# Graph network of four layers on one core: order of the closing units, the engine of the row checks, the place of four low halves, and the order of 16 bias matmuls

## The chip, the cores and the metric

One core of a Trainium2 chip. The metric is the device time of one execution in microseconds, the median of three runs. TensorE (PE) does the matmuls, VectorE (DVE) and ScalarE (ACT) empty PSUM and do the elementwise work, GpSimd (POOL) does elementwise work between SBUF tiles, and SyncE (SP) issues the DMAs.

## What is computed

`x` has 8 batches of 2048 nodes with 64 features. `adj` is a 2048 x 2048 matrix with the same value in all non-zero places of a row (each row is divided by its count). Each of four layers has the form `x = layernorm(x + f(x, adj))`:

```
# layer 0: weights and bias of each node from an embedding of 16 numbers
w = einsum('nd,dkio->nkio', embedding, weight);  b = einsum('nd,do->no', embedding, bias)
x_g = (x, A x, 2 A (A x) - x);                   out = einsum('bnki,nkio->bno', x_g, w) + b
# layer 1: attention over adj > 0.5; layer 2: (A + I)(x W' + b) / degree
# layer 3: three steps of v = relu([v, A v] W1' + b1) W2' + b2, then the last layernorm
```

## The kernel before

**Data.** `X` holds the nodes in 16 tiles of 128 rows, with four column chunks `c` of 128 (two batches each). A unit (c, j) is a chunk and four node tiles, 128 x 512 values. `Bm` holds the pattern of `adj` in fp8, in 2 x 16 tiles of 128 x 1024: the left columns first, then the right ones. Matmuls take each value as two f16 halves. The high half is written by ACT and the low half by DVE (helper `lo_half`, line 1190 in the profile) or POOL.

**Order.** The whole program is one list of steps, `HEAD + MIDDLE + TAIL`, written by hand. Each engine walks the same list and does its own part of each step, so within an engine the list sets the order, and between engines semaphores do. `last_order` builds the last part with `at(k, ...)`, work beside product k, and `on(h, ...)`, work ahead of half slot h. `between` puts work between the two quarters of a half slot.

**Head.** While `adj` arrives, `tensor_head` multiplies all 16 left tiles into eight PSUM banks (lines 795 to 802). Then step `("R", jt)` makes DVE turn right tile jt into the pattern (`edges`, line 1187). Step `("E1", n)` has ACT write the high half of left unit n (line 1009) and DVE the low half. Product `P1` (`quarter`, line 743) takes unit 8 and later: its quarter q waits for right tiles up to 4q + 3, and its first quarter also for the low half that frees its bank. `("nb",)` is 16 f32 matmuls (line 816) of 16 rows each, which give the bias of each node: eight for h = 0 with operands at partition 0, into bank 4, and eight for h = 1 at partition 64, into bank 5. DVE copies both banks. `("wn",)` follows on PE (lines 830 and 832) and DVE. `("xs", g)` centres x on DVE and adds the biases on POOL. `t1` on POOL (line 1698) writes halves that product `P2` waits for.

**Row checks.** The fast path holds only for an `adj` of the stated kind, so the kernel checks it. For each of 16 row tiles, step `("chk", it)` has ACT sum the pattern (Copy with a running sum) and DVE take the maximum of the raw row, 2048 f32 values, negated into `nr`. Step `("sgn", it)` has ACT take Sign(row + nr) with a running sum. The next row tile is fetched once that is done. `chk` stands beside every other product and `sgn` beside the next. `flags` on DVE compares it all.

**Layer 3 and the end.** The products of its last two steps are formed as seven slots per pair of blocks (line 916). Slots 1, 4, 5 and 6 end a unit. `("V", n, s, jj)` empties a slot: for slot 6 ACT does a Relu (line 1035) and DVE the high half (line 1182) and the low half. Then `F` (lines 728 to 730, 12 matmuls) makes the unit's contribution to x and DVE adds it (four instructions of 128 x 128). For the norm, `sq` sums squares: ACT with eight sums and reads (`summed_by_act`) or ACT with one Square and DVE with a reduce. `var3` is a small DVE step and a square root on ACT (helper line 1035), `rs3` five small DVE steps (lines 1481 to 1485), and `out` a multiply of 128 x 512 on POOL (`by_gpsimd`) or DVE (both line 1203) and a 256 KB DMA issued by SP (line 706). The last eight units in order are (2,0), (2,1), (3,2), (3,3), (2,2), (2,3), (3,0), (3,1), numbered 8 to 15 by `order3`.

The list before, from `("M", 7, 6, 0)` on: V(7,6,0), F(2,3), sq(2,3), M(7,6,2), F(3,0), M(7,6,3), V(7,6,1), sq(3,0), var3 and rs3 of (2,2) with (2,3), F(3,1), sq(3,1), var3 and rs3 of (3,0), the outs of (2,2), (2,3), (3,0), then var3, rs3 and out of (3,1). Just ahead of it stand F(2,2), sq(2,2), var3 and rs3 of (3,2) with (3,3), and their outs.

## Time and profile before

| | before |
|---|---|
| median of three runs | 1060.19 us (1059.72 to 1060.27) |
| the profiled execution | 1058.48 us, its span 1056.7 us |
| PE busy | 1026.8 us, 97% |
| DVE busy | 727.3 us, 69% |
| POOL busy | 536.2 us, 51% |
| ACT busy | 422.6 us, 40% |
| mean granted TensorE clock | 0.994 |

Some 1.8 us of the profiled execution lie outside its span. A busy share is a mean over stages; what bounds a stage is read in that stage. PE's busy time counts overlapping matmuls once, and its ends are modelled.

### The profile page before, as it was taken

What the parts mean: (1) busy time and instruction counts of PE and PEld (TensorE: products, weight loads), DVE (VectorE), ACT (ScalarE), POOL (GpSimd) and SP (SyncE); (2) the same over time, 40 slices, a digit from 0 to 9 for tenths busy, and PEclk for the clock granted to TensorE, in tenths of its full rate; (3) what the DMA queues carried; (4) which work ended last, traced back from release to release, by engine and by line L of the source; (5) the groups of instructions that cost most, each with busy time, mean ns of one, the idle gap of its engine ahead of it and who ended that gap; (6) DMA issues with size and microseconds to landing.
All of it is one profiled execution on the core that took longest, in us unless ns stands there. A gap on an engine that the chain in (4) does not pass through costs nothing.

```text
span 1056.7 us, 18773 instructions
## 1 busy us (share of the span) xinstructions
PE 1026.8 (97%) x6922; PEld 493.9 (47%) x6922; DVE 727.3 (69%) x1751; ACT 422.6 (40%) x1081; POOL 536.2 (51%) x623
## 2 busy tenths in 40 slices
PE   7999999999999999999999999999999999999994
PEld 3446444434443444344345555555554545455542
DVE  4876565677557765775674899988667776767556
ACT  4632233333334343534423555446345422231633
POOL 0004487547456766775671757578864233323300
PEclk9999999999999999999999999999999999999998
DMA  9930000000000000000010121212212100000022
GB/s 368 399 122 1 1 2 2 1 2 1 1 1 2 1 2 2 1 1 2 1 41 1 41 81 41 81 41 81 80 41 81 40 1 1 3 1 22 21 60 60
DMA packets 14657, 45.65 MB, mean 43 GB/s; under 512 B 960, under 2 KB 9280, under 8 KB 10080
## 3 DMA queue, kind: packets, MB, share of 16 engines
q1 hardware_dynamic: 14560, 44.39, 11.4%
q8 instruction: 57, 0.93, 0.4%
q14 instruction: 40, 0.33, 0.1%
HBM read 40.19 MB, written 4.19 MB: 42 GB/s over the span
## 4 chain that ended last, share of the span: by engine, by line
PE 82%; DVE 8%; POOL 3%; issue 3%; ACT 2%; DMA 2%; SPq 0%; POOLq 0%; ACTq 0%; DVEq 0%
PE PS L743 33%; PE PS L872 20%; PE PS L916 18%; PE PS L728 2%; DMA BW<-at_in 2%; PE PS L729 2%; PE PS L730 2%; DVE BW L1187 1%; DVE T L1190 1%; PE PS L737 1%; ACT T L1035 1%; PE PS L735 1%; PE PS L736 1%; DVE X L1190 1%; PE PS L897 1%
## 5 line engine op out<-in xcount | busy, mean ns | idle before, releaser
L743 PE MATMUL PS<-BW,S 128*128 128x512 fp8e4 x1792 | 403.4, 379 | 4.0 <-DVE T L1190 2.0
L743 PEld LDWEIGHTS PS<-BW,S 128*128 128x128 f16 x1792 | 169.5, 98 | 210.7 <-issue 15.8
L872 PE MATMUL PS<-WZ,R 64*128 64x512 f16 x1536 | 198.7, 377 | 3.3 <-ACT T L1035 3.3
L1035 ACT ACTIVATE T<-PS,SM 128x128 f32<-128x128 f32 x384 | 112.5, 365 | 207.3 <-DVE X L1190 137.6
L1735 POOL TENSOR_TENSOR T<-T 128x128 f32<-128x128 f32 (+1 forms) x192 | 126.8, 660 | 125.3 <-ACT T L1035 114.8
L1190 DVE SCALAR_TENSOR_TENSOR X<-PS,SM,X 128x128 f32<-128x128 f32 x320 | 109.7, 343 | 38.0 <-PE PS L872 37.8
L872 PEld LDWEIGHTS PS<-WZ,R 64*128 64x128 f16 x1536 | 69.2, 94 | 107.2 <-issue 25.4
L916 PE MATMUL PS<-BW,S 128*128 128x512 fp8e4 x512 | 115.4, 379 | 0.1
L872 PE MATMUL PS<-WZ,T 64*128 64x512 f16 x768 | 103.8, 376 | 0.0
L1735 POOL TENSOR_TENSOR S<-R,S 128x512 f16<-128x512 f32 x48 | 57.5, 1212 | 89.3 <-ACT S L1035 89.3
L1190 DVE SCALAR_TENSOR_TENSOR T<-PS,SM,T 128x128 f32<-128x128 f32 x256 | 87.9, 343 | 21.6 <-PE PS L872 21.6
L1735 POOL TENSOR_TENSOR T<-R,T 128x512 f16<-128x512 f32 x42 | 49.6, 1187 | 80.2 <-DVE T L1182 55.0
L1757 POOL TENSOR_TENSOR BW<-BW 128x512 fp8e4<-128x512 fp8e4 x64 | 75.4, 1203 | 0.0
L916 PEld LDWEIGHTS PS<-BW,S 128*128 128x128 f16 x512 | 49.2, 98 | 55.5 <-issue 0.5
L916 PE MATMUL PS<-BW,T 128*128 128x512 fp8e4 x320 | 72.8, 379 | 0.0
L1035 ACT ACTIVATE R<-PS,cs 128x512 f32<-128x512 f32 x48 | 32.7, 681 | 98.3 <-PE PS L737 68.1
L1735 POOL TENSOR_TENSOR X<-X,T 128x128 f32<-128x128 f32 x128 | 59.4, 464 | 10.0
L728 PE MATMUL PS<-hat,T 128*128 128x128 f16 x320 | 56.8, 219 | 3.9 <-DVE T L1190 3.9
L1193 DVE TENSOR_REDUCE T<-T 128x8 f32<-128x512 f32 x32 | 21.9, 686 | 55.8 <-ACT T L1035 55.8
L795 PE MATMUL PS<-BW,S 128*128 128x512 fp8e4 x240 | 53.7, 388 | 5.5 <-DVE BW L1187 5.5
L872 PEld LDWEIGHTS PS<-WZ,T 64*128 64x128 f16 x768 | 37.4, 94 | 45.5
L730 PE MATMUL PS<-hat,T 128*128 128x128 f16 x320 | 56.8, 219 | 0.0
(217 smaller groups left out, 1505.3 us busy)
## 6 DMA issues: line engine op xcount, KB each, us to landing
WZ<-a_in SPq DMA_DIRECT2D x16, 1024.0 KB, 4.8
BW<-at_in SPq DMA_DIRECT2D x8, 1024.0 KB, 18.5
R<-at_in SPq DMA_DIRECT2D x7, 1024.0 KB, 13.3
out<-X SPq DMA_DIRECT2D x16, 256.0 KB, 2.3
X<-x_in SPq DMA_DIRECT2D x3, 1024.0 KB, 20.7
T<-w_in SPq DMA_DIRECT2D x1, 1536.0 KB, 15.5
R<-at_in SPq DMA_DIRECT2D x2, 512.0 KB, 4.9
SM<-sm_in SPq DMA_DIRECT2D x1, 520.5 KB, 17.9
```

Source lines behind the costliest of these rows:

```text
L728: e.matmul(ok, th, hat[:, 0, kind, :], start=True, stop=False)
L729: e.matmul(ok, tl, hat[:, 0, kind, :], start=False, stop=False)
L730: m = e.matmul(ok, th, hat[:, 1, kind, :], start=False, stop=True)
L743: m = e.matmul(o, stile(h, t, c), Bm[:, t, block(j)], start=(t == 0 and h == 0), stop=(last and t == NT - 1 and h == 1))
L795: e.matmul(bank(2 * c + j), stile(h, jt, c), Bm[:, jt, block(j)], start=(jt == 0 and h == 0), stop=False)
L872: m = e.matmul(bank(b0 + q), halves[kd][zh][r, :], WZ[r, wh, kd, block(g)], start=(i == 0), stop=(i == 8))
L916: m = e.matmul(o, half_of(n, what, h, q % 2)[:, t, :], b[:, 4 * (q % 2) + t, :], start=(s in (0, 1, 3) and q % 2 == 0 and t == 0 and h == ...
L1035: return e.activation(o, i, f, **kw)
L1190: return e.scalar_tensor_tensor(out=o, in0=a, scalar=s, in1=b, op0=f, op1=g)
L1193: return e.tensor_reduce(o, i, op=f, axis=AX.X, apply_absolute_value=absolute, negate=negate)
L1735: return e.tensor_tensor(o, a, b, f)
L1757: e.tensor_tensor(o, a, b, f, saturate=False).then_inc(s_bt, 1)
```

## The change

1. `HEAD`: the low halves of left units 0 to 3 (`E1` 0 to 3) move up between right tiles R9 to R14. Before, they stood after R12 and R13.
2. `nb`: the 16 bias matmuls are issued in turns, h = 0 then h = 1 for each t, instead of eight and eight. Both wait for `s_u1` 6 at the start, and both signals come with the last pair.
3. Row checks: DVE's maximum is dropped. `nr` is the negated known value of the row. ACT sums Relu(row + nr) into `over` ahead of the Sign in step `sgn`.
4. The end: roots and variances are separate steps (`var3` on DVE, `root3` on ACT), always for two units. The list from half 54 on is reordered: var3 and root3 of (3,2) with (3,3) stand ahead of F(2,2); var3 of (2,2) stands ahead of V(7,6,1), its root3 and rs3 behind it; (3,0) and (3,1) share one var3, root3 and rs3. Unit 13 (2,3) is summed by Square and a DVE reduce, and the outs of units 10 and 11 move from DVE to POOL.

The rest of the diff renames `tmp16` to `over` and adds a semaphore `s_over`.

```diff
@@ -83,8 +83,9 @@
-HEAD = ([("R", jt) for jt in range(13)]
-        + [("E1", 0), ("E1", 1), ("R", 13), ("E1", 2), ("E1", 3), ("R", 14), ("R", 15), ("dg",)]
+HEAD = ([("R", jt) for jt in range(9)]
+        + [("E1", 0), ("R", 9), ("R", 10), ("E1", 1), ("R", 11), ("R", 12), ("E1", 2), ("R", 13), ("E1", 3), ("R", 14), ("R", 15)]
+        + [("dg",)]
         + pieces("P1", 0) + [("E1", 4), ("E1", 5), ("wm",), ("E1", 6), ("E1", 7), ("E1", 8)]
@@ -218,16 +219,21 @@
     for n, s, jj, h in ((6, 1, 0, 33), (6, 1, 1, 34), (6, 4, 0, 41), (6, 4, 1, 42), (6, 5, 0, 43), (6, 5, 1, 44), (6, 6, 0, 44),
-                        (6, 6, 1, 45), (7, 1, 0, 47), (7, 1, 1, 48), (7, 4, 0, 52), (7, 4, 1, 53), (7, 5, 0, 54), (7, 5, 1, 55)):
+                        (6, 6, 1, 45), (7, 1, 0, 47), (7, 1, 1, 48), (7, 4, 0, 52), (7, 4, 1, 53)):
         on(h, ("F", *ending(n, s, jj)), ("sq", 3, *ending(n, s, jj)))
-    for n, s, h in ((6, 1, 36), (6, 4, 43), (6, 5, 46), (6, 6, 47), (7, 1, 49), (7, 4, 54), (7, 5, 56)):
+    def outs(n, s):
+        return [("out", *ending(n, s, jj)) for jj in range(2)]
+
+    for n, s, h in ((6, 1, 36), (6, 4, 43), (6, 5, 46), (6, 6, 47), (7, 1, 49)):
         u = ending(n, s, 0)
-        on(h, ("var3", *u, 2), ("rs3", *u, 2), ("out", *u), ("out", *ending(n, s, 1)))
-    u, v = ending(7, 6, 0), ending(7, 6, 1)
-    between[55] = [("F", *u)]
-    w = half[56]
-    half[56] = [("sq", 3, *u), *w[:2], ("F", *v), ("sq", 3, *v), ("var3", *u, 1), ("rs3", *u, 1), *w[2:], ("out", *u),
-                ("var3", *v, 1), ("rs3", *v, 1), ("out", *v)]
+        on(h, ("var3", *u), ("root3", *u), ("rs3", *u), *outs(n, s))
+
+    r, (u, v), (x, y) = ending(7, 4, 0), [ending(7, 5, jj) for jj in range(2)], [ending(7, 6, jj) for jj in range(2)]
+    on(54, ("var3", *r), ("root3", *r), ("F", *u), ("sq", 3, *u), ("rs3", *r), *outs(7, 4))
+    on(55, ("F", *v))
+    between[55] = [("F", *x), ("sq", 3, *v), ("var3", *u)]
+    on(56, ("root3", *u), ("rs3", *u), *outs(7, 5), ("F", *y), ("sq", 3, *x), ("sq", 3, *y), ("var3", *x), ("root3", *x),
+       ("rs3", *x), *outs(7, 6))
     for g in range(2):
...
@@ -629,14 +636,14 @@
                     held[buf] = x[1:]
-                elif x[0] in ("var", "var3"):
+                elif x[0] in ("var", "root3"):
                     VARN[norm_key(x)] = len(VARN)
...
-        REDN = {x: n for n, x in enumerate(y for y in SQN if y[0] < 3 or not order3(*y[1:]) < 14)}
+        REDN = {x: n for n, x in enumerate(y for y in SQN if y[0] < 3 or order3(*y[1:]) > 12)}
         ORDER3 = [ending(n, s, jj) for n in (6, 7) for s in ENDS for jj in range(2)]
@@ -645,11 +652,11 @@
-            return order3(c, j) < 8 or order3(c, j) in (12, 13)
+            return order3(c, j) < 8 or 10 <= order3(c, j) < 14
...
-            return order3(c, j) < 14
+            return order3(c, j) < 13
@@ -810,12 +817,13 @@
                     e.wait_ge(s_b2b, 2)
-                    for h in range(2):
-                        e.wait_ge(s_u1, 5 + h)
-                        for t in range(8):
+                    e.wait_ge(s_u1, 6)
+                    for t in range(8):
+                        for h in range(2):
                             m = e.matmul(bank(4 + h)[:, t * C:t * C + C], embt[h][:, t * 128:(t + 1) * 128], nbias[h],
                                          start=True, stop=True)
-                        m.then_inc(s_nbm, 1)
+                            if t == 7:
+                                m.then_inc(s_nbm, 1)
                 elif kind == "wm":
@@ -1083,12 +1091,14 @@
                         e.wait_ge(s_sq, SQN[L, c, j])
+                        if order3(c, j) == 15:
+                            e.wait_ge(s_red, REDN[(3, *ORDER3[13])] + 1)
                     elif SQPREV[L, c, j] is not None:
...
                     fn(four(sq_buf(L, c, j)), xpart(c, j), ACT.Square).then_inc(s_sq, 1)
-                elif kind in ("var", "var3"):
+                elif kind in ("var", "root3"):
                     L, c, j = (*norm_key(step), 0)[:3]
-                    m = step[3] if L == 3 else 1
+                    m = 2 if L == 3 else 1
                     e.wait_ge(s_var, VARN[norm_key(step)] + 1)
@@ -1167,13 +1177,16 @@
                     if it:
-                        e.wait_ge(s_cnt, it)
+                        e.wait_ge(s_over, it)
                     fn(junk, Bm[:, it, :], ACT.Copy, accum_out=cnt[:, it:it + 1]).then_inc(s_cnt, 1)
                 elif kind == "sgn":
+
                     it = step[1]
-                    e.wait_ge(s_nr, it + 1)
-                    if it:
-                        e.wait_ge(s_sign, it)
+                    e.wait_ge(s_land, 16 * (it + 1))
+                    e.wait_ge(s_nr, 1)
+                    e.wait_ge(s_cnt, it + 1)
+                    fn(junk, rowt, ACT.Relu, bias=nr[:, it:it + 1], accum_out=over[:, it:it + 1]).then_inc(s_over, 1)
+                    e.wait_ge(s_over, it + 1)
                     fn(rowt, rowt, ACT.Sign, bias=nr[:, it:it + 1], accum_out=sg1[:, it:it + 1]).then_inc(s_sign, 1)
...
@@ -1466,18 +1479,19 @@
                 elif kind == "var3":
-                    c, j, m = step[1:]
-                    if summed_by_act(c, j):
-                        e.wait_ge(s_sq, SQN[3, c, j + m - 1] + 1)
-                    else:
-                        e.wait_ge(s_red, REDN[3, c, j] + 1)
+                    c, j = step[1:]
+                    for i in (j, j + 1):
+                        if summed_by_act(c, i):
+                            e.wait_ge(s_sq, SQN[3, c, i] + 1)
+                        else:
+                            e.wait_ge(s_red, REDN[3, c, i] + 1)
                     r = order3(c, j) // 2
                     e.wait_ge(*((s_n[1], 16) if r < 2 else (s_n[3], 2 * r - 2)))
-                    ts(e, st_part(3, c, j, 2, m), st_part(3, c, j, 0, m), 1 / 64, 1e-5 * 4096, ALU.mult, ALU.add).then_inc(s_var, 1)
+                    ts(e, st_part(3, c, j, 2, 2), st_part(3, c, j, 0, 2), 1 / 64, 1e-5 * 4096, ALU.mult, ALU.add).then_inc(s_var, 1)
                 elif kind in ("rs", "rs3"):
...
                     e.wait_ge(s_sd, VARN[norm_key(step)] + 1)
-                    s0, s1, s2 = (st_part(L, c, j, k, step[3] if L == 3 else 1) for k in range(3))
+                    s0, s1, s2 = (st_part(L, c, j, k, 2 if L == 3 else 1) for k in range(3))
                     fc(e.reciprocal(s1, s1))
@@ -1633,6 +1647,7 @@
                 elif kind == "rows":
+                    ts(e, nr, rmax, -1.0, None, ALU.mult).then_inc(s_nr, 1)
                     ts(e, col(cRow0), i16[:, 0:1], LAM, None, ALU.mult)
@@ -1655,10 +1670,6 @@
                     scaled(e, c, j).then_inc(s_n[3], 1)
-                elif kind == "chk":
-                    it = step[1]
-                    e.wait_ge(s_land, 16 * (it + 1))
-                    red(e, nr[:, it:it + 1], rowt, ALU.max, negate=True).then_inc(s_nr, 1)
                 elif kind == "flags":
@@ -1668,10 +1679,9 @@
                     fc(e.tensor_tensor(sg1, sg1, q1, ALU.not_equal))
-                    fc(e.tensor_tensor(nr, nr, rmax, ALU.add))
-                    fc(ts(e, nr, nr, 0.0, None, ALU.not_equal))
-                    fc(e.tensor_tensor(nr, nr, sg1, ALU.add))
-                    red(e, sums[:, 0, 1:2], nr, ALU.add).then_inc(s_cw, 1)
+                    fc(ts(e, over, over, 0.0, None, ALU.not_equal))
+                    fc(e.tensor_tensor(over, over, sg1, ALU.add))
+                    red(e, sums[:, 0, 1:2], over, ALU.add).then_inc(s_cw, 1)
                 elif kind == "verdict":
```

## Rows read from the trace of the kernel before

**Rows 1.** The page's part 1: busy time, share of the span, instructions.
```profile
PE 1026.8 (97%) x6922; PEld 493.9 (47%) x6922; DVE 727.3 (69%) x1751; ACT 422.6 (40%) x1081; POOL 536.2 (51%) x623
```

**Rows 2.** Windows: stretch, length, busy of PE, PEld, DVE, ACT, POOL, granted clock, DMA.
```profile
530.00:870.00 340.00, 340.00 (x2220) 179.70 (x2218) 263.96 (x498) 155.44 (x235) 202.48 (x174) 1.00 0.14 50
1036.40:1056.70 20.30, 5.99 (x47) 3.11 (x44) 13.26 (x45) 5.01 (x23) 2.08 (x2) 0.76 0.27 77
```

**Rows 3.** Timeline of PE around the end of the left products: start, length, what.
```profile
62.34 0.38 PE L802 MATMUL PS<-BW,S 128*128 128x512 fp8e4 x1
64.68 7.08 PE L743 MATMUL PS<-BW,S 128*128 128x512 fp8e4 x32 [1.96 <-DVE T L1190]
```

**Rows 4.** Chain that ended last: start, length, what; then ACT's timeline there.
```profile
56.19 7.83 DVE BW L1187 x13
...
136.39 3.45 PE PS L743 x16
139.84 3.99 PE PS L872 x36
...
59.73 2.06 ACT L1009 ACTIVATE T<-PS 128x512 f16<-128x512 f32 x4 [8.78 <-PE PS L802]
```

**Rows 5.** Timeline of PE and of its weight loads (PEld): the biases, one layer-0 pair.
```profile
79.73 3.39 PE L816 MATMUL PS<-T 16*128 16x64 f32 x32
79.73 3.25 PEld L816 LDWEIGHTS PS<-T 16*128 16x128 f32 x32 [0.42 <-issue]
...
132.22 0.10 PEld L872 LDWEIGHTS PS<-WZ,T 64*128 64x128 f16 x2
```

**Rows 6.** PE's timeline at the first P2; a window of the granted clock.
```profile
105.59 7.08 PE L743 MATMUL PS<-BW,S 128*128 128x512 fp8e4 x32 [0.24 <-POOL S L1698]
...
85.00:85.50 0.50, 0.50 (x8) 0.50 (x6) 0.47 (x2) 0.00 (x0) 0.00 (x0) 0.50 0.00 0
```

**Rows 7.** Instructions that touch the tile ra: durations ns min/median/max.
```profile
L1193 DVE TENSOR_REDUCE ra<-WZ x16: 2269/2276/2286, 582.0 to 834.9; 128x1 f32<-128x2048 f32 x16
L1035 ACT ACTIVATE WZ<-WZ,ra x16: 1985/1990/2004, 592.4 to 837.2; 128x2048 f32<-128x2048 f32 x16
```

**Rows 8.** Timeline at the end, from V(7,6,0) to F(3,0): ACT, DVE, PE.
```profile
1036.26 0.67 ACT L1035 ACTIVATE R<-PS,cs 128x512 f32<-128x512 f32 x1
...
1033.08 1.12 DVE L1190 SCALAR_TENSOR_TENSOR X<-PS,R,X 128x128 f32<-128x128 f32 x4
...
1036.38 0.25 DVE L1481 RECIPROCAL T<-T 128x16 f32<-128x16 f32 x1 [2.11 <-ACT T L1035]
...
1037.51 1.49 DVE L1203 TENSOR_TENSOR X<-X,T 128x512 f32<-128x512 f32 x2
1038.91 0.42 DVE L1182 TENSOR_SCALAR T<-R 128x512 f16<-128x512 f32 x1
...
1040.21 0.22 PE L728 MATMUL PS<-hat,T 128*128 128x128 f16 x1 [1.86 <-DVE T L1190]
```

**Rows 9.** Timeline of DVE and POOL while POOL multiplies an earlier unit.
```profile
1001.79 2.23 POOL L1203 TENSOR_TENSOR X<-X,T 128x512 f32<-128x512 f32 x2 [9.31 <-DVE T L1485]
...
1003.49 0.56 DVE L1183 TENSOR_SCALAR T<-T 128x16 f32<-128x16 f32 x1
```

**Rows 10.** Timeline of the last steps: PE, DVE, POOL.
```profile
1045.47 0.22 PE L728 MATMUL PS<-hat,T 128*128 128x128 f16 x1 [2.06 <-DVE T L1190]
...
1047.29 1.12 DVE L1190 SCALAR_TENSOR_TENSOR X<-PS,R,X 128x128 f32<-128x128 f32 x4
...
1049.11 0.69 DVE L1193 TENSOR_REDUCE T<-WZ 128x8 f32<-128x512 f32 x1 [0.69 <-ACT WZ L1035]
...
1051.81 0.17 DVE L1183 TENSOR_SCALAR T<-T 128x8 f32<-128x8 f32 x1
...
1053.29 0.69 DVE L1203 TENSOR_TENSOR X<-X,T 128x512 f32<-128x512 f32 x1
...
1047.46 2.23 POOL L1203 TENSOR_TENSOR X<-X,T 128x512 f32<-128x512 f32 x2 [38.29 <-DVE T L1485]
```

More of the change, by code:

```diff
@@ L305, in gnn_kernel @@
         PS = ctx.enter_context(nc.psum_tensor("PS", [128, 4096], F32))
-        rmax, cnt, nr, sg1, q64, q1, cw, r64, tmp16, cw2 = (ra[:, k, :] for k in range(10))
+        rmax, cnt, nr, sg1, q64, q1, cw, r64, over, cw2 = (ra[:, k, :] for k in range(10))
         rows = SM[:, 0:256].rearrange("p (k c) -> p k c", c=C)
@@ L351, in gnn_kernel @@
         s_mx = sem("s_mx")
+        s_over = sem("s_over")
         s_t2 = sem("s_t2")
@@ L1341, in vector_head @@
                 elif kind == "bounds":
-                    vc(e.tensor_tensor(tmp16, q1, rmax, ALU.mult))
-                    vc(ts(e, tmp16, tmp16, -1.0, None, ALU.add))
-                    red(e, fl[:, 0:1], tmp16, ALU.max, True)
+                    vc(e.tensor_tensor(over, q1, rmax, ALU.mult))
+                    vc(ts(e, over, over, -1.0, None, ALU.add))
+                    red(e, fl[:, 0:1], over, ALU.max, True)
                     red(e, fl[:, 1:2], q1, ALU.max)
@@ L2126, in vector_slow @@
                 fetch(1)
-                vc(red(e, tmp16[:, it:it + 1], row_a, ALU.add))
-            vc(ts(e, tmp16, tmp16, 1.0, None, ALU.add))
-            vc(e.reciprocal(tmp16, tmp16))
+                vc(red(e, over[:, it:it + 1], row_a, ALU.add))
+            vc(ts(e, over, over, 1.0, None, ALU.add))
+            vc(e.reciprocal(over, over))
             for it in range(NT):
                 vc(e.tensor_tensor(tmp, E[:, it, :], V[:, it, :], ALU.add))
-                vc(stt(e, X[:, it, :], tmp, tmp16[:, it:it + 1], X[:, it, :], ALU.mult, ALU.add))
+                vc(stt(e, X[:, it, :], tmp, over[:, it:it + 1], X[:, it, :], ALU.mult, ALU.add))
                 norm(it)
```

## The prediction

> **What bounds the kernel now.** I read the busy shares first: PE is busy for 97% of the span, the next engine for 69% [rows 1]. So time can come out only where PE stands idle, where PE itself does fewer or better packed matmuls, or behind its last matmul. Then I read busy time by stretch. Beside the row checks, from 530 to 870 us, PE is busy 340.00 of 340.00 us, DVE 264 and ACT 155 [rows 2]: no time can be won there by relieving DVE, only lost by holding PE up. From 1036.4 us on PE is busy 5.99 of 20.30 us [rows 2], so the end is set by a chain through DVE, ACT and POOL. Then I read PE's timeline where its waits are: 1.96 us behind the left products [rows 3], 1.86 us ahead of F(3,0) [rows 8], 2.06 us ahead of F(3,1) [rows 10].
>
> **Part 1, the low halves between right tiles.** PE issues its last left matmul at 62.34, and at a pitch of 0.216 us (3.45 / 16 [rows 4]) it is free at 62.56. P1 starts at 64.68, on a DVE low half [rows 3]. DVE had 13 right tiles ahead of it, from 56.19 for 7.83 us, 0.602 us each [rows 4]. The high half is no hindrance: ACT writes all four from 59.73 to 61.79 [rows 4]. With nine right tiles ahead, and a low half as long as a tile, the first low half ends as the tenth item, at 56.19 + 6.02 = 62.21: PE no longer waits at 62.56. What is late next: the fourth quarter of P1 needs R15. PE reaches it at 62.56 + 24 x 0.216 = 67.74. DVE has 16 tiles and four low halves to do, so R15 ends at 56.19 + 20 x 0.602 = 68.23, with the signal 68.28. P1 then ends at 68.28 + 8 x 0.216 = 70.01 instead of 64.68 + 32 x 0.216 = 71.59. The gain is **1.6 us**, with 0.54 us of a new wait in it. The tiles R9 to R14 are taken later than before and R15 at its old time, so no landing can come too late. Low halves 4 and 5 keep their place in DVE's queue. Bounds: 1.3 to 2.1, the latter if the new wait were not there.
>
> **Part 2, the biases in turns.** The 32 matmul records (two per f32 matmul) take some 3.3 us, and the weight loads are busy for 3.25 of it, 0.102 us each [rows 5]: loads set the pace, since only 64 columns stream. Layer 0 already has two row groups in turns: its 36 matmuls of 64 x 512 take 3.99 us, 0.111 each, where a 128-row one takes 0.216 [rows 4], so two run at once. The loads of such a pair run at once too: two of them lie within 0.10 us [rows 5]. The new order has rows 0 to 15 and 64 to 79 in turns, with a bank of their own each. If that holds for f32, half of 3.25 goes, 1.6 us. Against it, DVE's first copy no longer runs beside the second half of the matmuls. The f32 matmuls of wn cover most of the two copies (0.6 us each, the pitch of a DVE item in [rows 4]), and I charge 0.1. Net **1.5 us**; the bounds are -0.1 (loads stay one after the other) and 1.6. I take the upper end because the row that is nearest, the loads of a pair, shows the overlap.
> The Trainium skill, "TensorE: Matmul & The Clock Gate", section "LDWEIGHTS (loading the stationary operand)", says that a load's time goes by its columns and not by its rows. By that alone, 16-row loads one after another would gain nothing. The same page's "Part 3: Packing small matmuls" says that a load overlaps matmuls in flight when the row groups differ. By this rule the gain would be as above.
>
> Does it reach the end? Behind the biases PE is at half clock for a while (granted 0.50 at 85 us [rows 6]), yet at the first P2 it waits 0.24 us for POOL's halves [rows 6]. POOL's and DVE's chain from the biases sets that point, and the chain starts at the biases, so it moves with parts 1 and 2. A PE that ran faster in between would gain nothing more. If PE's slow stretch came longer, more than 0.24 us of it would cost. Nothing behind is tied to a fixed time: the DMAs of the inputs are over by then, and the next ones wait for the last product of layer 0.
>
> **Part 3, the row checks.** DVE loses 16 x 2.28 = 36.4 us. ACT gains 16 Relu with a sum: the Sign over the same 2048 values takes 1.99 us [rows 7], and with the read of the sum I take 2.1 (bounds 2.0 and 2.3), 34 us in all. PE has no idle time there [rows 2], so the gain is **0**. The cover for the cost: ACT goes from 155 to 189 busy of 340 us, one Relu and Sign (4.2 us) in every second product of some 8.5 us. Queued behind them on ACT is the emptying of that same product. It falls due a product later, and PE wants the bank three products later. The tile's load waits for the Sign, as before, but now it is ACT that waits for the landing, a product later than DVE did. The fetch has more time, not less. Cost **0**, bounds 0 to 4 us.
> The rule against this part stands in the Trainium skill, "ScalarE: Activation LUTs", section "Rules for kernel authors": relu and max belong on VectorE and not on ScalarE. By the rows DVE's maximum is 0.3 us slower than ACT's pass [rows 7], so here the rule saves nothing; its sum would be 0 as well.
>
> **Part 4, the end.** Before, ACT took the root of (3,2) behind eight sums of (2,2), so DVE's rs3 started at 1036.38, its two outs at 1037.51 ran 1.49 us, and only then came the high half of V(7,6,0), at 1038.91, though its Relu was over at 1036.93 [rows 8]. F(3,0) followed at 1040.21, 1.30 us behind the start of the high half [rows 8].
> After: var3 stands ahead of the adding of F(2,2) (1033.08, 1.12 us [rows 8]), which ends at some 1034.3. The root is taken beside it. rs3 takes 1.13 us (1036.38 to 1037.51 [rows 8]), until 1035.4. POOL has the outs, 2.23 us for two [rows 9], until 1037.65. The high half could start at 1036.95. But while POOL multiplied an earlier unit until 1004.02, a small DVE step took 0.56 us, until 1004.05, instead of 0.17 [rows 9, 10]: DVE's step waited for POOL's to end. So I let the high half start in effect at 1037.55 and F(3,0) at 1037.55 + 1.30 = 1038.85, a gain of 1.36. Without the collision PE's own end at 1040.21 - 1.86 = 1038.35 [rows 8] would be the limit, a gain of 1.86.
> V(7,6,1) follows PE at its old distance, so F(3,1) starts at 1045.47 - 1.36 = 1044.11 [rows 10]. DVE has time for what moved in between: two addings of 1.12, a reduce of 0.69 and var3, 3.0 us, between 1038.7 and 1042.8. Then rs3 of (2,2) runs while PE does F(3,1), until 1045.1, and the adding of F(3,1) starts at 1045.1 instead of 1047.29 [rows 10]. From there, by the old distances: reduce 1.82 us later (1047.29 to 1049.11 [rows 10]), at 1046.9; it ends at 1047.5; var3, root and rs3 take 1.48 (1051.81 to 1053.29 [rows 10]), 1.5 with twice the columns; the first out starts at 1049.05 and the last 0.80 later (1.49 - 0.69 [rows 8, 10]), at 1049.85. Before, it started at 1053.29. The gain is **3.4 us**. What goes is one chain of roots and the outs of (3,2) and (3,3) on DVE. POOL's outs of (2,2) and (2,3) end at 1045.1 + 2.23 = 1047.35, just ahead of var3; if they are later, the small steps wait for them, up to 0.4 us. Bounds 3.0 to 3.95.
>
> **The sum.** 1.6 + 1.5 + 0 + 3.4 = 6.5 us, out of the profiled execution's 1058.48 (span 1056.7 and 1.8 around it): 1052.0. The median of the three runs stands 1.71 above that execution, so the time is 1060.19 - 6.5 = **1053.7**. With the ends of the parts: 1.3 - 0.1 - 4 + 3.0 = 0.2 (1060.0) and 2.1 + 1.6 + 3.95 = 7.65 (1052.5).
>
> **Rivals.** (a) The f32 loads stay one behind the other. For it: the loads of two f32 passes of one matmul overlap nothing at 0.102 us each [rows 5]. Part 2 gives -0.1: 1055.3. (b) Slower: ACT becomes late beside the products. Each Relu is 2.1 us in a strict queue, and where PE's next operand or bank has less slack than that, PE waits up to 2.1 us. It decides from the fourth of the 16 tiles on (4 x 2.1 = 8.4 > 6.5). With five tiles: 1053.7 + 10.5 = 1064.2. Against it: ACT is busy less than half of the stretch, and PE never waited there [rows 2]. (c) At the end POOL and DVE collide more than I let them: the high half, the reduces and the last small steps each wait for an out, and part 4 gives 1.0: 1056.1. For it: the two rows of the collision [rows 9]. (d) The head's gain is lost again, since POOL's chain meets work that did not move: 1060.19 - 3.4 = 1056.8. Against it: PE's wait of 0.24 us shows that chain and PE to be in step [rows 6].
>
> **Chances.** Forecast 0.55, (a) 0.20, (b) 0.05, (c) 0.12, (d) 0.08. The range from 1052.0 to 1057.2 takes in the forecast with its bounds, (a), (c) and (d), and leaves out (b) and mixtures. A measurement of this kernel tells some 0.2% (2.1 us) from no change. Only (b) is above; with mixtures between: faster 0.91, same 0.04, slower 0.05.
>
> **What would show it.** Right: P1 starts near 62.6 with a wait of about 0.5 us ahead of its last quarter; the bias matmuls take 1.7 us; PE still has no idle time beside the row checks, and ACT some 34 us more; F(3,0) starts about 3.1 + 1.4 us earlier than before, the last out 3.1 + 3.4. Wrong: bias matmuls of 3.3 us (a), PE waits behind ACT between 520 and 870 us (b), DVE steps of 0.5 to 1.1 us instead of 0.2 at the end (c), a longer wait for POOL between 100 and 130 us (d). The prediction would be most wrong if an order that I took from distances in the old trace had a wait in it that the old trace hid.

## The result

| | before | after |
|---|---|---|
| median | 1059.34 us (1058.27 to 1060.27, 6 runs) | 1052.67 us (1051.79 to 1053.16, 6 runs) |
| ratio | | 0.9939 (0.9927 to 0.9950) |
| the profiled execution | 1058.48 us, span 1056.7 | 1052.66 us, span 1050.9 |
| PE, DVE, ACT, POOL busy | 1026.8, 727.3, 422.6, 536.2 us | 1023.4, 690.4, 453.4, 538.1 us |
| mean granted TensorE clock | 0.994 | 0.996 |

The changed kernel is faster by 6.7 us in the medians and by 5.8 us between the two profiled executions. Forecast were 1053.7 us and a gain of 6.5. Of the 1.0 us between 1053.7 and the measured 1052.67, 0.85 lie in the starting value: the six runs of the kernel before have a median of 1059.34, and the forecast started at the 1060.19 of the first three.

Lines of the changed kernel stand some 7 to 14 lower in the file (L743 is L750 now, L816 is L823, L872 is L880, L1190 is L1203, L1203 is L1216, L1035 is L1043). The page's busy times, then windows behind the biases, beside the row checks and at the end (stretch, length, busy of PE, PEld, DVE, ACT, POOL, granted clock, DMA share, GB/s), against [rows 1, 2]:

```profile
PE 1023.4 (97%) x6922; PEld 490.9 (47%) x6922; DVE 690.4 (66%) x1728; ACT 453.4 (43%) x1097; POOL 538.1 (51%) x625
```

```profile
80.00:81.00 1.00, 1.00 (x13) 0.76 (x12) 0.37 (x1) 0.00 (x0) 0.00 (x0) 1.00 0.00 0
...
84.00:85.00 1.00, 1.00 (x10) 0.55 (x8) 0.80 (x3) 1.00 (x3) 0.00 (x0) 1.00 0.00 0
...
530.00:865.00 335.00, 335.00 (x2183) 177.30 (x2178) 225.25 (x470) 185.26 (x260) 199.51 (x173) 1.00 0.14 51
1031.00:1050.90 19.90, 8.88 (x67) 4.71 (x65) 13.06 (x41) 5.38 (x23) 4.17 (x4) 0.79 0.27 80
```

PE is as full as before beside the row checks, though ACT has 30 us more there (forecast 34) and DVE 39 us less, 36.4 of them the sixteen maxima [rows 2, 7]. What became shorter is the head and the end. The head, in PE's timeline (start, length, what, idle before and its releaser), against [rows 3, 5, 6]; the line with PEld is of the weight loads:

```profile
62.65 0.38 PE L809 MATMUL PS<-BW,S 128*128 128x512 fp8e4 x1
62.86 5.34 PE L750 MATMUL PS<-BW,S 128*128 128x512 fp8e4 x24
68.72 1.90 PE L750 MATMUL PS<-BW,S 128*128 128x512 fp8e4 x8 [0.52 <-DVE BW L1200]
70.46 0.38 PE L831 MATMUL PS<-SM,T 128*128 128x128 f32 x2
...
78.60 2.00 PE L823 MATMUL PS<-T 16*128 16x64 f32 x32
...
78.59 1.86 PEld L823 LDWEIGHTS PS<-T 16*128 16x128 f32 x32 [0.42 <-issue]
...
80.53 1.12 PE L838 MATMUL PS<-T,ones 128*128 128x512 f32 x2
...
103.13 7.08 PE L750 MATMUL PS<-BW,S 128*128 128x512 fp8e4 x32 [1.93 <-POOL S L1708]
110.14 0.82 PE L880 MATMUL PS<-WZ,R 64*128 64x512 f16 x6
```

The wait of 1.96 us ahead of P1 is gone, and one of 0.52 stands ahead of its last quarter (the other traces with this head have 0.23 or none). The biases take 1.93 us (78.60 to 80.53) instead of 3.32. The granted clock stays at 1.00, 2.4 GHz, behind them, where it was 0.50 before [rows 6]; and the wait for POOL's halves at the first P2 is 1.93 us instead of 0.24.

What POOL's halves wait for matters below. DVE reduces the two f32 products of `wn` that PE makes behind the biases, and a chain through ACT, DVE and POOL leads from there to the halves. DVE's two reductions and POOL's halves, in the kernel before and in the changed one, and the granted clock over `wn` in the kernel before:

```profile
84.21 1.09 DVE L1193 TENSOR_REDUCE cs<-PS 128x4 f32<-128x512 f32 x2 [0.37 <-PE PS L830]
104.20 2.50 POOL L1698 TENSOR_TENSOR S<-T,S 128x512 f16<-128x512 f32 x2
```

```profile
81.83 1.01 DVE L1206 TENSOR_REDUCE cs<-PS 128x4 f32<-128x512 f32 x2
101.74 2.49 POOL L1708 TENSOR_TENSOR S<-T,S 128x512 f16<-128x512 f32 x2
```

```profile
83.00:84.00 1.00, 1.00 (x4) 0.49 (x3) 0.69 (x1) 0.00 (x0) 0.00 (x0) 1.00 0.00 0
84.00:85.00 1.00, 1.00 (x7) 0.68 (x6) 0.79 (x2) 0.00 (x0) 0.00 (x0) 0.62 0.00 0
```

Both times POOL's halves start 18.90 us behind the end of the second reduction (85.30 and 82.84), and P2 starts 1.39 us behind their start. All twelve traces that keep the order of these steps have 18.9.

The end, in the timelines of ACT, DVE, POOL and PE, against [rows 8 to 10]:

```profile
1030.77 0.21 ACT L1043 ACTIVATE T<-T 128x16 f32<-128x16 f32 x1 [1.79 <-DVE T L1196]
...
1031.68 0.25 DVE L1495 RECIPROCAL T<-T 128x16 f32<-128x16 f32 x1
...
1034.43 0.93 DVE L1195 TENSOR_SCALAR T<-R 128x512 f16<-128x512 f32 x1 [1.66 <-ACT R L1043]
...
1043.40 1.47 DVE L1206 TENSOR_REDUCE T<-WZ 128x8 f32<-128x512 f32 x2
...
1046.54 1.49 DVE L1216 TENSOR_TENSOR X<-X,T 128x512 f32<-128x512 f32 x2
...
1032.85 2.23 POOL L1216 TENSOR_TENSOR X<-X,T 128x512 f32<-128x512 f32 x2 [26.19 <-DVE T L1499]
...
1036.23 0.22 PE L735 MATMUL PS<-hat,T 128*128 128x128 f16 x1 [0.39 <-DVE T L1203]
...
1041.49 0.22 PE L735 MATMUL PS<-hat,T 128*128 128x128 f16 x1 [2.06 <-DVE T L1203]
```

The root of (3,2) is taken at 1030.77, beside the adding of F(2,2), and its reciprocal no longer waits. PE waits 0.39 us ahead of F(3,0) instead of 1.86. Between the first f32 matmuls of V(7,6,0), at 1032.64, and F(3,0) there are now 3.59 us.

### The profile page after: what moved, and what is told of

Read it like the earlier page. It is cut to its first block, busy times and chain, and to the rows that moved or that the text cites. A ratio compares the mean times of both kernels' runs of the same rounds, so it can differ in the third digit from the quotient of the medians.

```text
span 1050.9 us, 18768 instructions
## 1 busy us (share of the span) xinstructions
PE 1023.4 (97%) x6922; PEld 490.9 (47%) x6922; DVE 690.4 (66%) x1728; ACT 453.4 (43%) x1097; POOL 538.1 (51%) x625
## 4 chain that ended last, share of the span: by engine, by line
PE 84%; DVE 9%; POOL 2%; ACT 2%; DMA 2%; issue 1%; SPq 0%; POOLq 0%; ACTq 0%; DVEq 0%
PE PS L750 34%; PE PS L880 21%; PE PS L924 18%; DMA BW<-at_in 2%; PE PS L735 2%; PE PS L737 2%; PE PS L736 2%; DVE BW L1200 1%; DVE T L1203 1%; DVE X L1203 1%; PE PS L744 1%; PE PS L742 1%; PE PS L743 1%; ACT T L1043 1%; PE PS L725 1%
## 5 line engine op out<-in xcount | busy, mean ns | idle before, releaser
L750 PE MATMUL PS<-BW,S 128*128 128x512 fp8e4 x1792 | 403.5, 379 | 4.3 <-POOL S L1708 1.9
L750 PEld LDWEIGHTS PS<-BW,S 128*128 128x128 f16 x1792 | 169.6, 98 | 211.0 <-issue 15.9
L1043 ACT ACTIVATE T<-PS,SM 128x128 f32<-128x128 f32 x384 | 112.5, 365 | 206.9 <-DVE X L1203 137.7
L880 PE MATMUL PS<-WZ,R 64*128 64x512 f16 x1536 | 198.5, 377 | 3.1 <-ACT T L1043 3.1
L1203 DVE SCALAR_TENSOR_TENSOR X<-PS,SM,X 128x128 f32<-128x128 f32 x320 | 109.9, 344 | 38.7 <-PE PS L880 38.5
L880 PEld LDWEIGHTS PS<-WZ,R 64*128 64x128 f16 x1536 | 69.2, 94 | 106.8 <-issue 25.4
L880 PE MATMUL PS<-WZ,T 64*128 64x512 f16 x768 | 103.8, 376 | 0.0
L1203 DVE SCALAR_TENSOR_TENSOR T<-PS,SM,T 128x128 f32<-128x128 f32 x256 | 88.0, 344 | 21.2 <-PE PS L880 21.2
L1043 ACT ACTIVATE R<-PS,cs 128x512 f32<-128x512 f32 x48 | 32.7, 681 | 98.7 <-PE PS L744 68.7
L1043 ACT ACTIVATE WZ<-WZ,ra 128x2048 f16<-128x2048 f32 (+1 forms) x32 | 63.9, 1996 | 0.5
L1195 DVE TENSOR_SCALAR T<-R 128x512 f16<-128x512 f32 x48 | 31.5, 657 | 47.5 <-ACT R L1043 46.6
L735 PE MATMUL PS<-hat,T 128*128 128x128 f16 x320 | 56.8, 219 | 2.4 <-DVE T L1203 2.4
L880 PEld LDWEIGHTS PS<-WZ,T 64*128 64x128 f16 x768 | 37.4, 94 | 45.5
## 6 DMA issues: line engine op xcount, KB each, us to landing
BW<-at_in SPq DMA_DIRECT2D x8, 1024.0 KB, 18.3
SM<-sm_in SPq DMA_DIRECT2D x1, 520.5 KB, 18.3
```

The source lines that it names most:

```text
L735: e.matmul(ok, th, hat[:, 0, kind, :], start=True, stop=False)
L750: m = e.matmul(o, stile(h, t, c), Bm[:, t, block(j)], start=(t == 0 and h == 0), stop=(last and t == NT - 1 and h == 1))
L880: m = e.matmul(bank(b0 + q), halves[kd][zh][r, :], WZ[r, wh, kd, block(g)], start=(i == 0), stop=(i == 8))
L1043: return e.activation(o, i, f, **kw)
L1195: return e.tensor_scalar(o, i, s1, None, o1)
L1203: return e.scalar_tensor_tensor(out=o, in0=a, scalar=s, in1=b, op0=f, op1=g)
```

## The experiments

Four kernels have one part of the change each. The kernel before has a median of 1058.80 us beside them (29 runs, 1057.56 to 1060.65).

### Part 1 alone

```diff
-HEAD = ([("R", jt) for jt in range(13)]
-        + [("E1", 0), ("E1", 1), ("R", 13), ("E1", 2), ("E1", 3), ("R", 14), ("R", 15), ("dg",)]
+HEAD = ([("R", jt) for jt in range(9)]
+        + [("E1", 0), ("R", 9), ("R", 10), ("E1", 1), ("R", 11), ("R", 12), ("E1", 2), ("R", 13), ("E1", 3), ("R", 14), ("R", 15)]
+        + [("dg",)]
```

> The kernel before with part 1 alone (low halves of left units 0 to 3 between right tiles). My theory: P1 starts when the left products end, waits about 0.5 us ahead of its last quarter, and all behind it moves by 1.4 to 1.6 us: ratio 0.9985 to 0.9987. Rival (the head's gain is lost again at POOL's chain): P1 starts earlier but the first layer-0 matmul does not, 0 us: ratio 1.000.

Measured: 1057.68 us (11 runs), ratio 0.9988 (0.9979 to 0.9997): 1.3 us by the ratio, with 0.3 to 2.2 in the interval. In its profiled execution (span 1056.0) the biases start 1.70 us earlier than before, at 78.03, but the first product of layer 0 starts only 0.25 us earlier, at 112.35. By the timelines of PE, DVE and POOL and two windows:

```profile
78.03 3.71 PE L817 MATMUL PS<-T 16*128 16x64 f32 x32
81.67 2.08 PE L831 MATMUL PS<-T,ones 128*128 128x512 f32 x2
...
84.64 0.42 DVE L1194 TENSOR_REDUCE cs<-PS 128x2 f32<-128x256 f32 x1 [0.16 <-PE PS L833]
...
103.95 2.50 POOL L1699 TENSOR_TENSOR S<-T,S 128x512 f16<-128x512 f32 x2
```

```profile
81.00:82.00 1.00, 1.00 (x5) 0.88 (x5) 0.22 (x1) 0.00 (x0) 0.00 (x0) 0.50 0.00 0
...
86.00:87.00 1.00, 1.00 (x12) 1.00 (x11) 0.59 (x3) 1.00 (x4) 0.00 (x0) 0.50 0.00 0
```

PE was busy without a gap, and its clock fell to 0.50 (1.2 GHz) while it did the f32 matmuls; it stayed there until past 87. So the biases take 3.64 us instead of 3.32, and DVE's second reduction ends 3.39 us behind them (85.06) instead of 2.25. That is 1.46 of the 1.70 us, and POOL's halves start 0.25 us earlier than before. PE itself was as late: it goes from P1 into P2, at 105.34, without a wait, just when the halves let it. So the gain of the order is there up to the biases, and in this execution the clock takes most of it, on PE's way and on POOL's.

### Part 2 alone

```diff
-                    for h in range(2):
-                        e.wait_ge(s_u1, 5 + h)
-                        for t in range(8):
+                    e.wait_ge(s_u1, 6)
+                    for t in range(8):
+                        for h in range(2):
...
```

> The kernel before with part 2 alone (bias matmuls in turns). My theory: they take 1.9 us instead of 3.3, and the first P2 moves by about 1.3 us, since POOL's chain starts behind the biases: ratio 0.9987 to 0.9989. Granted clock stays at 1.00 from 80 to 90 us, where before it fell to 0.50; PE's saving from that (some 1.7 us) only makes its wait for POOL longer. Rival: the saving of the clock comes on top, 3 us in all, ratio 0.997.

Measured: 1056.92 us (11 runs, 1056.32 to 1057.61), ratio 0.9983 (0.9974 to 0.9992): 1.8 us, between the 1.3 expected and the rival's 3. The biases and the first P2 in PE's timeline:

```profile
79.97 2.00 PE L816 MATMUL PS<-T 16*128 16x64 f32 x32
...
104.49 7.08 PE L743 MATMUL PS<-BW,S 128*128 128x512 fp8e4 x32 [1.92 <-POOL S L1699]
```

The matmuls gain the same 1.39 us (79.97 to 81.90). The clock is 1.00 in every window behind them, and all 11 runs have a mean clock of 0.995 or 0.996. The kernel before has 0.992 to 0.996 in its 29: the seven at 0.992 took 1059.16 to 1060.65 us, the six at 0.996 took 1057.97 to 1058.50. In between the two overlap (1057.56 to 1059.92 at 0.994). So much of its spread of 3 us goes with the clock, and with part 2 alone the spread is 1.3 us.

### Part 3 alone

The edit is that of the row checks in the diff, where ACT's Relu with a running sum takes the place of DVE's maximum:

```diff
+                    fn(junk, rowt, ACT.Relu, bias=nr[:, it:it + 1], accum_out=over[:, it:it + 1]).then_inc(s_over, 1)
+                    e.wait_ge(s_over, it + 1)
...
-                    red(e, nr[:, it:it + 1], rowt, ALU.max, negate=True).then_inc(s_nr, 1)
```

> The kernel before with part 3 alone (row checks on ScalarE). My theory: DVE 36 us less, ACT 31 to 34 us more, no change of the time, ratio 0.9998 to 1.0002. Rival (ACT late beside the products): PE waits between 560 and 860 us, 1.0005 to 1.01.

Measured: 1058.81 us (11 runs), ratio 1.0002 (0.9993 to 1.0011). PE is busy for 340.00 us of 340.00 from 530 to 870, ACT for 187.75 instead of 155.44. The part is worth nothing and costs nothing, within 1 us. At the first P2, PE waits 1.11 us for POOL and starts 0.67 us later than in the kernel before, though the biases started 0.25 earlier: here the clock fell to 0.50 at 83, over `wn`, and the second reduction ended 3.18 us behind the biases instead of 2.25.

### Part 4 alone

```diff
+    on(54, ("var3", *r), ("root3", *r), ("F", *u), ("sq", 3, *u), ("rs3", *r), *outs(7, 4))
...
+    between[55] = [("F", *x), ("sq", 3, *v), ("var3", *u)]
+    on(56, ("root3", *u), ("rs3", *u), *outs(7, 5), ("F", *y), ("sq", 3, *x), ("sq", 3, *y), ("var3", *x), ("root3", *x),
+       ("rs3", *x), *outs(7, 6))
...
```

> The kernel before with part 4 alone (the end). My theory: F(3,0) starts 1.4 to 1.5 us earlier, the last out 3.4 us, the end 3.3 us: ratio 0.9968 to 0.9970. Rival (the end also rests on an idler DVE ahead of it, from part 3): less than 2.5 us, ratio above 0.9976.

Measured: 1055.76 us (7 runs, 1054.92 to 1056.72), ratio 0.9971 (0.9960 to 0.9982): 3.1 us. F(3,0) waits 0.38 us, and the high half takes 0.93 us, as in the whole change. The four alone sum up to 0.0012 + 0.0017 - 0.0002 + 0.0029 = 0.0056, against 0.0061 together: within the intervals they add. Inside part 4 the outs and the root were tried singly, below; the one chain of roots for (3,0) and (3,1) and the Square with a reduce for (2,3) were not.

### The change with part 2 undone

The edit is the one of part 2, backwards, in the changed kernel. Beside this kernel and the next two, and beside the one of "What the first P2 waits for", the kernel before has a median of 1058.22 us (9 runs).

> The changed kernel with part 2 undone (bias matmuls eight and eight again, parts 1, 3 and 4 kept). My theory after the first four runs: the biases take 3.3 us again, and while they and the sums behind them run at 16 rows the clock falls to 0.50 near 81 us, as with part 1 alone, so PE and not POOL sets the first P2. 2.0 to 2.4 us slower than the changed kernel, ratio to before 0.9961 to 0.9966. Rival (the halved matmuls are all there is): 1.4 us slower, ratio 0.9952 to 0.9955.

Measured: 1054.89 us (5 runs, 1054.24 to 1055.37), ratio 0.9966 (0.9952 to 0.9980), against 0.9939 for the whole change: part 2 is worth some 2.9 us beside the others by the ratios, and 2.2 by the medians. In its trace the clock is at 0.68 from 82 to 83 and 0.50 until 85. What was expected of the place was wrong: PE still waits for POOL at P2, 0.82 us. P2 starts at 104.93, 1.80 us later than in the changed kernel: 1.39 for the matmuls and 0.54 since the second reduction ends 2.85 us behind the biases and not 2.31, less 0.14 since they start earlier. So the slow clock costs through `wn` and POOL's chain.

### In turns, but all on one row group

All 16 bias matmuls take rows 0 to 15, in turns between the two banks. The biases of the second half of the nodes are those of the first in it.

```diff
-                            m = e.matmul(bank(4 + h)[:, t * C:t * C + C], embt[h][:, t * 128:(t + 1) * 128], nbias[h],
+                            m = e.matmul(bank(4 + h)[:, t * C:t * C + C], embt[0][:, t * 128:(t + 1) * 128], nbias[0],
```

> The changed kernel, but both halves of the biases are computed from the operands at partitions 0 to 15, still in turns between the two banks (so the biases of nodes 1024 to 2047 are those of nodes 0 to 1023: that part is wrong). Theory (two row groups work at once): 3.3 us for the 16 matmuls, as before. Rival (changing the bank from matmul to matmul is what helps): 1.9 us, as in the changed kernel. Also: if the clock falls to 0.50 behind them, it goes with the single row group.

Measured: 1055.81 us, one run, so only its trace is read. The biases in PE's timeline, and a window behind them:

```profile
78.83 3.78 PE L823 MATMUL PS<-T 16*128 16x64 f32 x32
...
78.83 3.64 PEld L823 LDWEIGHTS PS<-T 16*128 16x128 f32 x32 [0.42 <-issue]
```

```profile
84.00:85.00 1.00, 1.00 (x3) 0.49 (x2) 0.34 (x1) 0.00 (x0) 0.00 (x0) 0.50 0.00 0
```

The order and the two banks give nothing: 3.71 us instead of 1.93, and the slow clock is back (0.77 from 82 to 83, 0.50 until 85). The two row groups carry the gain.

### The outs of (3,2) and (3,3) back on DVE

```diff
-            return order3(c, j) < 8 or 10 <= order3(c, j) < 14
+            return order3(c, j) < 8 or 12 <= order3(c, j) < 14
```

> The changed kernel, but the outs of units 10 and 11 stay on DVE. Theory: POOL is silent while the high half of V(7,6,0) runs, so that takes 0.43 us and not 0.93, but DVE has both outs (1.4 us) ahead of it or behind rs3: rs3 ends 1.2 us ahead of the Relu's end, so 0.2 to 0.3 us of the outs stick out. F(3,0) starts within 0.3 us of where it does in the changed kernel, the time within 0.3 us: ratio 0.9937 to 0.9942. Rival (moving the outs to POOL was what made the end faster): F(3,0) 1 us later or more.

Measured: 1052.09 us (5 runs, 1051.74 to 1052.41), ratio 0.9939 (0.9926 to 0.9953). DVE's timeline:

```profile
1032.73 1.49 DVE L1216 TENSOR_TENSOR X<-X,T 128x512 f32<-128x512 f32 x2
1034.37 0.43 DVE L1195 TENSOR_SCALAR T<-R 128x512 f16<-128x512 f32 x1
```

The two outs fit into DVE's idle time ahead of the high half, which takes 0.43 us again instead of 0.93, and PE doesn't wait ahead of F(3,0). Between the first matmul of V(7,6,0) and the last outs the trace has 0.5 us less (13.39 instead of 13.90); the runs tell no difference from the whole change. So with the early root POOL's share of the end brings nothing; what is left of the part is the order with its one chain of roots, and the way (2,3) is summed.

### The root of (3,2) late again

```diff
-    on(54, ("var3", *r), ("root3", *r), ("F", *u), ("sq", 3, *u), ("rs3", *r), *outs(7, 4))
+    on(54, ("var3", *r), ("F", *u), ("sq", 3, *u), ("root3", *r), ("rs3", *r), *outs(7, 4))
```

> The changed kernel with one step back in its old place: the root of (3,2) behind ACT's eight sums of (2,2) instead of ahead of F(2,2). Theory (the root behind the sums is what held the high half up before): rs3 starts 2.3 us later, the high half of V(7,6,0) waits for rs3 and for POOL's outs, F(3,0) starts 0.5 to 1.2 us later and the end with it. Rival (DVE's outs alone held it up, and POOL has them now): F(3,0) within 0.2 us of the changed kernel.

Measured: 1053.27 us (5 runs, 1052.87 to 1053.87), ratio 0.9944 (0.9930 to 0.9957), with 1059.15 for the kernel before (9 runs). The runs alone don't tell it from the whole change (0.9927 to 0.9950), so the trace is read, by DVE, POOL and PE:

```profile
1034.31 0.25 DVE L1495 RECIPROCAL T<-T 128x16 f32<-128x16 f32 x1 [2.19 <-ACT T L1043]
...
1035.77 1.42 DVE L1203 SCALAR_TENSOR_TENSOR T<-R,T 128x512 f16<-128x512 f32 x1
...
1035.48 2.61 POOL L1216 TENSOR_TENSOR X<-X,T 128x512 f32<-128x512 f32 x2 [28.47 <-DVE T L1499]
...
1037.34 0.22 PE L735 MATMUL PS<-hat,T 128*128 128x128 f16 x1 [1.14 <-DVE T L1203]
```

The reciprocal waits for the root as before the change, PE waits 1.14 us ahead of F(3,0) instead of 0.39, 0.75 more, and the collision moves to the low half: 1.42 us instead of 0.69. Its span is 1.1 us longer (1052.0 against 1050.9); 0.35 of that are there before V(7,6,0) starts. Against the kernel before (1.86) the wait is still 0.72 shorter: with the root late, the outs on POOL do help.

### Three and five Relus per tile

```diff
...
+                    for i in range(3):
+                        if it or i:
+                            e.wait_ge(s_over, 3 * it + i)
+                        fn(junk, rowt, ACT.Relu, bias=nr[:, it:it + 1], accum_out=over[:, it:it + 1]).then_inc(s_over, 1)
...
```

> The changed kernel with the Relu of each row check done three times (the sum in over is the last one's): 2 x 16 x 2.1 = 67 us more for ACT between 560 and 840 us. Theory (ACT has slack of more than a Relu beside each product): PE's waits there stay under 1 us, time within 1 us of the changed kernel. Rival (the change sits at the edge of ACT's slack, as my slower case had it): PE waits for each tile, 10 us or more.

> As the run before with five Relus: 134 us more for ACT, 8.4 us more in every second product of 8.5 us. Theory: here the slack ends, PE waits in sum 10 to 60 us between 560 and 870 us. It puts the point from which the slower case decides between 4.2 and 8.4 us of extra ACT work per tile. Rival (ACT is never on the path there): no wait even now.

Measured: three take 1077.21 us (4 runs), ratio 1.0166 (1.0151 to 1.0182), 24.5 us above the changed kernel; five take 1133.68 us (one run), 81 us above. The expectation for three was wrong by far; this is its rival. PE's waits in the kernel with three (line, released by: us in total, times, longest), and two windows:

```profile
PE PS L725 <- DVE S L1206: 7.3, 3, 6.5
PE PS L735 <- DVE T L1206: 5.4, 3, 3.1
PE PS L962 <- DVE gmh L1209: 3.2, 1, 3.2
```

```profile
530.00:900.00 370.00, 353.23 (x2248) 184.77 (x2245) 230.64 (x500) 252.27 (x326) 201.90 (x175) 0.98 0.13 46
720.00:760.00 40.00, 30.29 (x185) 15.66 (x181) 26.80 (x44) 29.35 (x38) 28.65 (x25) 0.87 0.14 50
```

ACT is busy for 252 of 370 us, 68%, and PE already loses 17 us there; where it stood idle, the clock was down to 0.87. Per tile, two Relus more (4.2 us) cost 24.5 / 16 = 1.5 us and four more (8.4 us) cost 81 / 16 = 5.1. So, by an estimate from these two means, ACT has a slack of some 3 us per tile (4.2 - 1.5 and 8.4 - 5.1) behind the one Relu of the change.

### What the first P2 waits for

At the first P2 POOL is late, and I asked why. In the changed kernel POOL multiplies through eight steps, those of xs 0 and xs 1 (L1717, L1719), ahead of the halves that PE wants, until 101.74. Here step xs 1 comes behind t1 3, so only the four of xs 0 are ahead, and the bounds step goes ahead of wm:

```diff
-        + pieces("P1", 0) + [("E1", 4), ("E1", 5), ("wm",), ("E1", 6), ("E1", 7), ("E1", 8)]
+        + pieces("P1", 0) + [("E1", 4), ("E1", 5), ("bounds",), ("wm",), ("E1", 6), ("E1", 7), ("E1", 8)]
...
-        + [("xs", 0), ("xs", 1)]
-        + pieces("P1", 2) + [("t1", 2), ("dx", 3), ("t1", 3), ("E1", 10), ("bounds",), ("xs", 2)]
+        + [("xs", 0)]
+        + pieces("P1", 2) + [("t1", 2), ("dx", 3), ("t1", 3), ("E1", 10), ("xs", 1), ("xs", 2)]
```

> The changed kernel with step bounds (a few small DVE steps and the all-reduce on POOL) moved ahead of wm, where both engines are idle, and xs 1 behind t1 3. Theory: PE's wait of 1.9 us for POOL ahead of the first P2 goes, and the all-reduce's 13.6 us on POOL lie in its idle time; what is late next is PE itself. 1.7 to 2.1 us faster than the changed kernel, ratio 0.9917 to 0.9923. Rival (the wait comes back at the first layer-0 units, where ACT and POOL sum): under 0.5 us, ratio above 0.9934.

Measured: 1051.04 us (5 runs, 1050.34 to 1051.56), ratio 0.9929 (0.9916 to 0.9943), against 0.9939 for the changed kernel: 1.1 us by the ratios, a little less than expected, 1.6 by the medians and 1.9 by the spans of the two traces. POOL's and PE's timelines:

```profile
97.26 2.27 POOL L1708 TENSOR_TENSOR S<-T,S 128x512 f16<-128x512 f32 x2
...
94.78 13.54 PE L750 MATMUL PS<-BW,S 128*128 128x512 fp8e4 x62
108.25 0.82 PE L880 MATMUL PS<-WZ,R 64*128 64x512 f16 x6
```

POOL's halves come at 97.26 instead of 101.74, PE goes from P1 into P2 without a gap, and layer 0 starts at 108.25 instead of 110.14: the 1.9 us of the spans are the whole wait of 1.93.

### The version beyond both

It takes that order, the outs of (3,2) and (3,3) on DVE, and a last out that doesn't wait for the one ahead of it.

```diff
-                    e.wait_ge(s_n[3], order3(c, j))
+                    e.wait_ge(s_n[3], min(order3(c, j), 14))
```

> The changed kernel with the bounds step early and xs 1 late, the outs of units 10 and 11 on DVE, and the last out not waiting for the one before it on the same engine. Theory: 1.9 us (no wait for POOL at the first P2), 0.5 us (no collision at the high half of V(7,6,0)) and 0.2 us add up: 2.4 to 2.7 us faster than the changed kernel, ratio 0.9912 to 0.9918, faster than both kernels. Rival (the two parts are not additive, or the gain at the last out is lost in the DMA): under 2 us.

Measured: 1049.90 us (4 runs, 1049.84 to 1050.35), ratio 0.9913 (0.9898 to 0.9929), with 1059.15 for the kernel before; span 1048.1. The last two outs:

```profile
1043.73 1.29 DVE L1216 TENSOR_TENSOR X<-X,T 128x512 f32<-128x512 f32 x2
```

It is 9.2 us faster than the kernel before and 2.8 faster than the changed one. Of the 2.8 us between the spans, 2.5 are there when layer 0 starts (107.67 instead of 110.14): the wait at P2, and 0.4 since in this execution the biases start earlier (78.23 instead of 78.60). 0.5 are the high half without a collision: from the first matmul of V(7,6,0) to the end it is 17.8 us instead of 18.3, and in the kernel with the outs back on DVE it was 17.7 already. 0.2 are lost in between. The last out brings nothing: the two take 1.29 us instead of 1.49, but from the start of the first to the end of the span it is 4.4 us as in the changed kernel. That part of the rival came true: what the last out gains is lost in the DMAs behind it.

## Why the prediction came out right

**Part 1, forecast 1.6.** The step was right in kind: P1 goes on at PE's own pitch behind the left products. From the last left matmul to the first f32 matmul behind P1's first piece it is 7.81 us (62.65 to 70.46) instead of 9.25, a gain of 1.44. In this execution the left products ended 0.31 us later than in that of the kernel before [rows 3], so that much of the gain is hidden in the comparison of the spans. That the new wait for R15 is 0.52 us (forecast 0.54) was luck: left products and R15 both came later here than in the old trace, and of the ten traces with this head only this one and that of the last kernel (0.23) have the wait at all. Over all traces that f32 matmul starts at 69.82 to 70.72 in the ten with the new head (mean 70.37) and at 71.35 to 71.83 in the four with the old (mean 71.64): 1.3 us, the lower end of the forecast's 1.3 to 2.1.

**Part 2, forecast 1.5.** The mechanism was right: with two row groups the 32 f32 loads are busy for 1.86 us instead of 3.25, and with one row group in turns between the banks for 3.64. Rival (a) falls. The size was a little off: a pair of loads takes 1.93 / 16 = 0.121 us, where I took 0.102 from a single one. The gain is 1.39 us, not 1.6, and the 0.1 for the copies is below what the trace tells. The Trainium skill's rule on row groups, "TensorE: Matmul & The Clock Gate", section "Part 3: Packing small matmuls", is that a load overlaps matmuls in flight only when the row group differs; the traces agree for f32 too, with these numbers. By the rule on columns of the same page's section "LDWEIGHTS (loading the stationary operand)" alone, the biases would have stayed at 3.3 us.

**The path from the biases to P2** was the step that failed in part. The prediction let POOL's chain start at the biases and follow them at a fixed distance, and so gave the clock nothing. In this pair of traces that held: PE came to P2 earlier, and all of that went into the wait for POOL (1.93 us instead of 0.24). But `wn`'s two f32 products, on PE, lie in that chain. Where the clock is 1.00 over them, DVE's second reduction ends 2.2 to 2.3 us behind the biases; where it fell in time to slow them it is 2.9 (part 2 undone), 3.2 (part 3 alone) and 3.4 us (part 1 alone, and one row group). So a term of 0.5 to 1.2 us, which depends on the execution, stood at nothing. PE waits for POOL at P2 in every trace with this order of the steps but that of part 1 alone, where the two come together. The condition that I did name, more than 0.24 us of a longer slow stretch of PE, is met in that trace, but it isn't the only way in which the clock costs.

The kernel before doesn't always look as in its one trace, where the clock fell only late in `wn`. Its runs at a mean clock of 0.992 take 1.6 to 2.2 us longer than those at 0.996, in each of three sets of runs; the changed kernel's six have 0.995 to 0.997. That would put the gain of the medians (6.7 us) above that of the two traces (5.8), and the worth of part 2 in the whole change (2.2 to 2.9 us) above its 1.39 of matmuls. No run of the kernel before at 0.992 was traced, so for those it is inferred.

**Does the head's gain reach the end?** Yes: P2 starts 2.46 us earlier, layer 0 too, and the first matmuls of V(7,6,0) start at 1032.64 instead of 1035.14, 2.50 earlier. 1.44 + 1.39 - 0.31 = 2.52. Rival (d) falls.

**Part 3, forecast 0.** Right: alone it measures 1.0002, and PE has no idle time there. Rival (b) falls, since PE waits for nothing that ACT is late with. But the reason that I gave, that ACT is busy less than half of the stretch, was too weak for what it had to carry. At 55% busy (185.26 of 335 us) nothing is lost, at 68% the kernel loses 24.5 us. What counts is the slack per tile: behind the change's one Relu some 3 us are left by the estimate above, and two Relus more (4.2 us) don't fit in them.

**Part 4, forecast 3.4.** F(3,0) gains 1.48 us of its own (3.98 with the head's 2.50), forecast 1.36. The collision came as forecast, on the same instruction: the high half takes 0.93 us, from 1034.43 to 1035.36, while POOL multiplies until 1035.08 (forecast a delay of 0.60, measured 0.50). The last out starts at 1047.34 (1046.54 + 0.80) instead of 1053.29, 5.95 us earlier, 3.45 of it its own. From that start to the end of the span, the out and its DMA, it is 3.56 us instead of 3.41, so the part gives 3.3 us; alone it measures 3.1. Rival (c) holds in kind, for the collision is real, but costs 0.5 us and not 2.4. In what I took for the source of the gain, the root was right and the outs were not: POOL's outs are worth nothing beside an early root, and DVE had the room for them. Taking the root late again cost F(3,0) 0.75 us, half of its 1.48. How much the one chain of roots and the Square of (2,3) carry is not shown singly.

**The sum.** 1.44 + 1.39 + 0 + 3.3 = 6.1, less the 0.31 by which the left products ended later, is the 5.8 us between the two traces. The forecast's 6.5 lies close to the medians' 6.7 with some luck: parts 1, 2 and 4 each gave a little less than forecast, and the medians hold a worth of the clock that the forecast put at nothing.

## What to carry to other kernels

Small f32 matmuls with few rows should alternate between row groups, as their loads then run at once, and here PE kept its clock as well. At an end that is a chain through several engines, start the short steps early (a root beside an adding) before moving bulk work to another engine: here the move to POOL gained nothing beside the early root, and the collision with a step of DVE cost 0.5 us. Judge room on an engine by the slack per period of its strict queue, not by its busy share, and look at the waits of the changed kernel: what the clock gave PE back had turned into most of a wait of 1.9 us, which moving two steps removed. When an engine seems off the critical path, look whether something that it makes stands in the chain that is on it, as `wn`'s products do here.
